# Graph layer on one core: the forward scan's result and a node tile's first residual sum in PSUM in place of SBUF

## What is computed

```
x1  = x + sigmoid(GAT(xn) + bias) + linear_attention(xn) * gate(xn) @ Wproj + bproj
xn2 = layernorm(x1)
out = x1 + xn2 + (FFN(xn2) * score, only for the top half of the nodes by score = xn2 @ wr + br)
```

## Time and profile before

| | |
|---|---|
| time, median of 3 runs | 1304.03 us (1302.03 to 1304.25) |
| the profiled execution, its own time | 1300.92 us |
| its span, first to last instruction | 1299.1 us |
| PE busy | 1033.9 us, 80% |
| DVE busy | 1011.7 us, 78% |
| POOL busy | 834.9 us, 64%, 832 gathers among it |
| ACT busy | 553.2 us, 43% |
| mean granted clock of TensorE | 0.887 of full speed |

### The profile page before, as it was taken

The page is one execution under the profiler, slowest core; times in us unless marked ns, Lnnn a source line. Parts: engine busy times, 40 slices in busy tenths (PEclk is TensorE's granted clock), DMA queues, the critical chain, the costliest instruction groups (busy, mean ns, idle before and its releaser), DMA issues.

```text
span 1299.1 us, 24124 instructions
## 1 busy us (share of the span) xinstructions
PE 1033.9 (80%) x5823; PEld 801.6 (62%) x5823; DVE 1011.7 (78%) x2620; ACT 553.2 (43%) x1169; POOL 834.9 (64%) x876
## 2 busy tenths in 40 slices
PE   4897578675887978779887787889788897788886
PEld 2685456543666756667666665667566675666665
DVE  4783666578778878788888888888788887888788
ACT  1234323133544535454453544535354553535521
POOL 1114666677777777777777777777777777777000
PEclk9898789866979988899888998989888988889789
DMA  9876566666666666656666666666656566666205
GB/s 353 300 153 156 177 186 178 190 161 179 155 161 162 173 164 167 175 157 172 164 166 169 161 172 159 165 160 167 175 154 171 160 168 162 165 163 160 54 1 198
DMA packets 158650, 218.64 MB, mean 168 GB/s; under 512 B 48937, under 2 KB 121437, under 8 KB 158605
## 3 DMA queue, kind: packets, MB, share of 16 engines
q0 software_dynamic: 39984, 110.94, 34.1%
q1 hardware_dynamic: 108976, 96.41, 25.7%
q10 hardware_dynamic: 9645, 10.78, 2.5%
HBM read 174.14 MB, written 43.88 MB: 168 GB/s over the span
## 4 chain that ended last, share of the span: by engine, by line
PE 33%; DVE 15%; issue 13%; POOL 13%; DMA 12%; ACT 2%; SPq 2%; DVEq 1%; POOLq 0%; ACTq 0%
POOL ring L708 13%; PE bank L1900 8%; DMA ring<-feat_d,idx 8%; PE bank L1865 7%; PE bank L1837 7%; DVE ring L1306 4%; PE bank L1816 3%; PE bank L1876 2%; PE bank L1988 2%; DMA parts_d<-wout 2%; PE bank L1825 2%; DVE xnT L1511 1%; PE bank L1699 1%; DMA lists<-dloc_d 1%; DVE lk L1266 1%
## 5 line engine op out<-in xcount | busy, mean ns | idle before, releaser
L708 POOL DMA_INDIRECT ring<-feat_d,idx x832 | 819.0, 984 | 285.5 <-issue 228.3
L1306 DVE TENSOR_TENSOR ring<-ring,bank 128x1024 f32<-128x1024 f32 x208 | 240.0, 1217 | 2.7 <-ACT bank L1579 2.7
L1865 PE MATMUL bank<-ring,hot 128*64 128x265 f32 x1664 | 213.0, 400 | 16.5 <-DVE ring L1306 16.1
L1900 PE MATMUL bank<-late,w_s 128*128 128x256 f32 x768 | 219.1, 443 | 0.4 <-ACT hT L1638 0.4
L1900 PEld LDWEIGHTS bank<-late,w_s 128*128 128x128 f32 x768 | 172.4, 229 | 31.1 <-ACT hT L1638 0.5
L1865 PEld LDWEIGHTS bank<-ring,hot 128*64 128x64 f32 x1664 | 143.7, 140 | 67.5 <-issue 18.2
L1579 ACT ACTIVATE bank<-diff 128x64 f32<-128x64 f32 x52 | 11.8, 228 | 399.3 <-DVE diff L1290 349.4
L1837 PE MATMUL bank<-w_s,hT 128*128 128x256 f32 x720 | 175.9, 400 | 1.2 <-ACT hT L1666 1.2
L1816 PE MATMUL bank<-ident,lk 128*16 128x128 f32 x208 | 43.0, 346 | 154.2 <-DVE lk L1266 154.2
L1837 PEld LDWEIGHTS bank<-w_s,hT 128*128 128x128 f32 x720 | 141.6, 202 | 22.4 <-ACT hT L1666 1.4
L1816 PEld LDWEIGHTS bank<-ident,lk 128*16 128x16 f32 x208 | 17.4, 102 | 170.7 <-DVE lk L1266 131.1
(11 more groups left out here) (268 smaller groups left out, 1620.3 us busy)
## 6 DMA issues: line engine op xcount, KB each, us to landing
parts_d<-zero SPq DMA_DIRECT2D x59, 265.0 KB
parts_d<-wout SPq DMA_DIRECT2D x208, 66.2 KB
lists<-dloc_d SPq DMA_DIRECT2D x104, 128.0 KB
ring<-feat_d,idx POOLq DMA_INDIRECT x832
parts<-parts_d SPq DMA_DIRECT2D x49, 265.0 KB
three<-in_x SPq DMA_DIRECT2D x49, 128.0 KB, 3.1
out<-xnT SPq DMA_DIRECT2D x5, 896.0 KB, 4.2
three<-in_x SPq DMA_DIRECT2D x15, 256.0 KB, 5.5
```

The lines of the kernel that those rows point to most:

```text
L708: pool.indirect_dma_start(out=ring[:, u * TI + q, 0:AW], out_offset=None, in_=feat_d, in_offset=bass.IndirectOffsetOnAxis(ap=idx[:, u, q:q ...
L1306: V.tensor_tensor(feats, feats, ex[:, g * TG:(g + 1) * TG, :].unsqueeze(3) .to_broadcast([P, TG, HEADS, HD]), ALU.mult).then_inc(S("scaled ...
L1865: mm = T.matmul(bank[2 + n][c * WIN:(c + 1) * WIN, 0:SW], hot[:, q, :], ring[:, u * TI + q, 0:SW], start=(j == 0), stop=(j == TG - 1))
L1900: mm = T.matmul(bank[6 + g][:, m % 2 * 2 * P:(m % 2 + 1) * 2 * P], w1_s[:, t, m * P:(m + 1) * P], xn2T[:, t, :], start=(t == 0), stop=(t = ...
```

## The change

The forward scan writes its result back over its input in bank 1, and the backward scan reads it there; the tile `forth` is no longer used in `maxima`. For all node tiles but the last three, x1 is held in `bk_t[:, 256:512]`, the other half of the projection's bank, in place of `sd`: L1385, L1389 and L1393 write it there, and L1389, L1393, L1395, L1348 and L1362 read it there. PE's guards of the bank move accordingly: `turn_scores` and `project` wait for `rest_made` (L1362 of the previous tile) in place of `proj_read`, and for `max_made` in place of `forth_made`. No instruction is added or taken away.

```diff
-                    V.tensor_tensor_scan(forth[:, :], brk[:, 0:GE], bk_t[0:TI, :], LOWEST, ALU.add, ALU.max
+                    V.tensor_tensor_scan(bk_t[0:TI, :], brk[:, 0:GE], bk_t[0:TI, :], LOWEST, ALU.add, ALU.max
                                          ).then_inc(S("forth_made"), 1)
                     dve.wait_ge(S("forth_made"), k + 1)
-                    V.tensor_tensor_scan(srow[:, :][:, ::-1], brk[:, 1:GE + 1][:, ::-1], forth[:, :][:, ::-1],
+                    V.tensor_tensor_scan(srow[:, :][:, ::-1], brk[:, 1:GE + 1][:, ::-1], bk_t[0:TI, :][:, ::-1],
                                          LOWEST, ALU.add, ALU.max).then_inc(S("max_made"), 1)
...
+                def first_sum(i, u):
+
+                    return sd[:, u, :] if isinstance(i, int) and i >= NT - 3 else bk_t[:, C:2 * C]
...
-                    V.tensor_scalar(to, sd[:, u, :], bn[:, u, 6:7], bn[:, u, 9:10], ALU.subtract, ALU.mult
+                    V.tensor_scalar(to, first_sum(i, u), bn[:, u, 6:7], bn[:, u, 9:10], ALU.subtract, ALU.mult
                                     ).then_inc(S("xn2_made"), 1)
...
-                    V.tensor_tensor(tile(xnT, i), sd[:, u, :], to, ALU.add).then_inc(S("rest_made"), 1)
+                    V.tensor_tensor(tile(xnT, i), first_sum(i, u), to, ALU.add).then_inc(S("rest_made"), 1)
...
+                    x1 = first_sum(i, u)
                     dve.wait_ge(S("proj_done"), i + 1)
-                    V.scalar_tensor_tensor(sd[:, u, :], bk_t[:, 0:C], rstd[:, bass.ds(i, 1)], prow[:, :], ALU.mult, ALU.add
+                    V.scalar_tensor_tensor(x1, bk_t[:, 0:C], rstd[:, bass.ds(i, 1)], prow[:, :], ALU.mult, ALU.add
...
-                    V.scalar_tensor_tensor(sd[:, u, :], sa[:, u, :], 0.5, sd[:, u, :], ALU.mult, ALU.add
+                    V.scalar_tensor_tensor(x1, sa[:, u, :], 0.5, x1, ALU.mult, ALU.add
...
-                    V.tensor_tensor(sd[:, u, :], sd[:, u, :], xs[:, u, :], ALU.add).then_inc(S("x1_made"), 1)
+                    V.tensor_tensor(x1, x1, xs[:, u, :], ALU.add).then_inc(S("x1_made"), 1)
                     dve.wait_ge(S("x1_made"), i + 1)
-                    V.bn_stats(bn[:, u, 0:6], sd[:, u, :]).then_inc(S("bn_made"), 1)
+                    V.bn_stats(bn[:, u, 0:6], x1).then_inc(S("bn_made"), 1)
...
                     if isinstance(k, int) and k <= LAG_SUM:
                         if k:
-                            pe.wait_ge(S("forth_made"), k)
+                            pe.wait_ge(S("max_made"), k)
                     else:
-                        pe.wait_ge(S("proj_read"), k - LAG_SUM)
+                        pe.wait_ge(S("rest_made"), k - LAG_SUM)
...
                 def project(i, u):
                     pe.wait_ge(S("prod_made"), i + 1)
-                    if not known_below(i, 1):
+                    if isinstance(i, int) and i > NT - 3:
                         pe.wait_ge(S("proj_read"), i)
+                    elif not known_below(i, 1):
+                        pe.wait_ge(S("rest_made"), i)
                     if not (isinstance(i, int) and i + LAG_SUM >= NI):
-                        pe.wait_ge(S("forth_made"), i + LAG_SUM + 1)
+                        pe.wait_ge(S("max_made"), i + LAG_SUM + 1)
```

## The result

| | before | after |
|---|---|---|
| median (lowest to highest) of 5 runs each | 1304.03 us (1302.03 to 1305.03) | 1288.86 us (1281.69 to 1289.61) |
| ratio after / before, 95% interval | | 0.9872 [0.9844, 0.9899] |
| the profiled execution, its own time | 1300.92 us | 1281.69 us |
| granted clock of that execution | 0.887 | 0.895 |

The change makes the kernel 1.28% faster, 15.2 us between the medians; the interval reaches from 13 to 20 us. The forecast was 1291.5 us, 1285 to 1298, with 91% for faster; it said 12.3 us. The profiled execution of after is the fastest of its five. The other four took 1283.97 to 1289.61 us; the clock was 0.895 in the two shortest and 0.889 or 0.890 in the other three. So its 19.2 us against the profiled execution of before are more than the change brings on average; where the time goes can still be read from it.

The account below looks back on a forecast made before the run. POOL's gathers were taken to pace the 44 steps, stretched by DVE instructions with two SBUF inputs. Removing 17.9 us gross less 5.6 coming back gave 12.3: 1304.0 - 12.3 = 1291.7, stated as 1291.5 us, range 1285 to 1298.

Parts of the forecast that it names:

- What bounds the kernel: In the 44 steps POOL issues gather after gather and hardly waits, so its 20.63 us a step is the loop's period.
- Part 1: Gathers starting under the backward scan L1277 are no longer stretched: 12.1 us in the steps plus 1.0 in the ramp.
- Part 2: Gathers starting under the tile sums L1348, L1393, L1362 and L1389 are no longer stretched: 4.8 us.
- Part 3: Gathers shift under L1332 and L1358 (3.2 us), L1358 starts later (1.2), POOL waits anew (1.2): 5.6 us back, 0 to 10.
- rival 4: Faster: phases of gathers against DVE fall well and only 1 us comes back, about 1287 us; 14%.
- Part 4: DVE durations: PSUM costs scans and sums nothing; L1348 goes from 415 to 480 ns, 3.0 us in all, hidden.
- Part 5: PE's moved guards in turn_scores and project are never the last wait, so they cost nothing.
- Rival 1: Slower: reading and writing one bank takes DVE two turns a column at L1274, L1385, L1389, L1393; about 1328 us; 4%.
- Rival 2: No change: the stretch comes with the scan's time, not its operands; only L1348's 2.1 us go, about 1302 us; 5%.
- Rival 3: Half: gathers slide far more into L1210, L1332 and L1358, 10 us come back, about 1296 us; 17%.

Follow-up runs that it names:

- after_plus: The changed kernel with two more DVE statistics instructions a step, whose output nobody reads; 1297.80 us on chip A, 0.9959 of the kernel before.
- scan_only_2: The kernel before with only the scans changed: forward result kept in PSUM, tile sums still in SBUF; 1293.72 us on chip A, ratio 0.9913.
- guards_only: The kernel before with only PE's waits as the change has them, every tile still in SBUF; 1301.48 us on chip A, ratio 0.9989.
- after_again: The changed kernel as it stands, run again on chip B; 1615.82 us, 1.0205 of the kernel before there.

## Why the prediction was right, point by point

**What bounds the kernel.** Right. POOL's gathers pace the 44 steps: in five of the six traces the window is the gathers' busy time plus 214 to 216 us of fixed gap, and only after_plus, made to run out of DVE's room, departs from it. The share of the span would have pointed at PE.

**Part 1, the scans, 13.1 us gross.** Right: in the 44 steps of scan_only_2 the stretched time is 12.4 us below the kernel before (8.1 below guards_only on the same chip), no gather over 1.21 us was left, and the ratio says 11.3 us, 7 to 15.

**Part 2, the tile sums, 4.8 us gross.** In the stretch of after 45 gathers start under L1352, L1394 and L1398 (none under L1366), and none is stretched, where 49 were in scan_only_2, by 4.2 us. Taken alone its time was not measured on a chip where POOL paces. One reading was wrong: L1348 doesn't have two SBUF tensors like the other three, but one, in a fast form. From PSUM, without that form, it stretches none.

**Part 3, what comes back, 5.6 us.** This is the term that was mis-sized, and why the forecast was 3 us short. By the medians 17.9 - 15.2 = 2.7 us came back, if the gross is taken as counted, and in the profiled execution, the fastest, nothing did. I had the gathers slide under L1332 and L1358 once the long stretches were gone. In scan_only_2 nothing slid. In after L1210, L1332, L1358 (now L1362) and L1328 hold 47 gathers, by 5.4 us, in place of 55 by 9.6: L1362 holds 4 in place of 17, L1332 7 in place of 13, L1210 15 in place of 22, and L1328 21 in place of 3, for 0.05 us each. All that is stretched is 6.0 us, where my terms leave 26.9 - 16.9 + 4.4 = 14.4. POOL's new waits came to less as well: above the fixed gap there are 1.3 us in place of 0.8, so 0.5 us for the 1.2 reckoned, and 1.04 of the 1.3 are one wait before a 15th gather.

Why the dot product came free can be followed in the positions of the gathers, though no run tests it alone. L1352 takes 0.13 us longer than L1348 did, so L1362 starts that much later. In the kernel before, the 17 gathers that L1358 holds start 104 to 155 ns after it, 13 of them at 104 to 111. In after, 7 gathers start 21 to 26 ns ahead of L1362 and 5 start 52 to 91 ns after it, and none of these is held; the 4 that are start 102 to 105 ns after it. So a gather has to start some way into the instruction to be held. At L1332 in after the edge lies between 44 ns (not held) and 45, at L1277 in the kernel before between 8 ns (not held) and 46. I had counted 0.065 us and reckoned that it holds each gather longer. Chance has a part too: in guards_only, with no operand moved, L1358 holds 9 gathers and L1332 9, and the window is 5.1 us shorter than in the kernel before. The 3 us that the forecast missed are no more than such phases do. The effect of a shift has no sign of its own; it depends on whether the next instruction moves over the gather's start or away from it. I had put the better case at 14% as rival 4, 1287, to which 1288.9 lies nearer (1.9 us) than to 1291.5 (2.6). That the time fell so near the forecast is in part luck: the gross was right, what comes back was not.

**Part 4, durations.** L1352 was to take 480 ns and takes 544, 46 x 0.064 = 2.9 us of DVE more than reckoned. Scans and sums were to cost nothing in PSUM and cost next to nothing: L1274 1216 ns for 1207, L1394 and L1398 429 and 432 for 427 and 425. Both were hidden. The wait at L1257 went to 17.7 us where I had said 22, 0.40 a step where I had said 0.5 to 0.6, but not because of them: 22 was 37.3 - 12.3 - 3.0, while the stretch became 18.7 us shorter in this execution, and 37.3 - 18.7 is 18.6. That leaves 0.9 us for the longer instructions. POOL's round shrank more than reckoned; DVE's own, with its waits for PE in it, is 19.8 us in both kernels (20.63 - 0.85 and 20.20 - 0.40).

Of the two pages weighed in the prediction: the 62 cycles that the Trainium skill ("VectorE: DVE Perf Modes", section "The TRN2 errata") adds for a PSUM source don't show in the scans and sums, which lost 9 ns at most. L1352 lost 130, twice that figure, and it is also the one that left a fast form; no run separates the two. The Trainium skill's inference in "SBUF — State Buffer", section "Who interferes with whom", that `tensor_tensor` didn't stall a DMA of GpSimd because descriptor generation needs the write interface, doesn't carry over to these gathers: scan_only_2, where only the scan's operand moved and PE's wait for it with it, has a longest gather of 1.20 us in the 44 steps, guards_only on the same chip one of 1.89.

**Part 5, the waits.** Right, by guards_only.

**The rivals.** Rival 1 (in-place PSUM takes a second turn for each column, 1328) falls by the rows of L1274 and L1398: 9 and 7 ns more where it wanted 527 and 264. Rival 2 (the time of the scan) falls by scan_only_2. Rival 3 (10 us come back) falls by part 3: 2.7 us by the medians.

**The size.** 15.2 us by the medians and 16.7 by the ratio (0.0128 x 1303), against 12.3. The two profiled executions differ by 19.2, of which the clock, 0.895 against 0.887, may hold some; how much wasn't separated.

## What to carry to other kernels

If GpSimd's indirect DMAs pace a loop, lay each gather beside what the vector engine had under way at its start: here an instruction with both inputs in SBUF held it until it ended, and moving one input to PSUM freed it, at 9 ns an instruction, or 130 where the instruction lost a fast form by it. The gross gains counted from the trace held here; what came back through shifted phases was mis-sized, so give that part a range of both signs, and expect it from any edit: 0.84 us of work a step, put into 0.85 us of room, cost 12 us. And read what paces the loop on the chip at hand: on four chips this loop waited for PE, and the gain was gone.

## What was not expected of the hardware

- Chips differ by some 22% for the same kernel: 1303 to 1304 us in the comparison of the prediction and on chip A, 1591 to 1609 on B to E, with a granted clock of 0.82 in place of 0.89 and waits called "remote" of 127 us on POOL alone, on one core that works by itself. Each chip was seen in one session, so it could also be the session. In the timeline of after_again PE's L1821 starts at 1225.38 us with 0.60 us of work, and DVE's L1274, which needs it, only at 1231.01. L1194, ahead of it in DVE's list, ended at 1229.58, and the last 1.43 us are its own wait:

```profile
1225.38 0.60 PE L1821 MATMUL bank<-ident,lk 128*16 128x128 f32 x4 [0.23 <-issue]
1231.01 1.22 DVE L1274 TENSOR_TENSOR_SCAN bank<-brk,bank 16x512 f32<-16x512 f32 x1 [1.43 <-remote]
```

- A second per-partition scalar, with its multiplication, costs L1352 60 ns on 256 columns, in PSUM and in SBUF alike.
- The gathers hold DVE as well. In the kernel before L1257, a copy of 128x16, takes 176 ns in the median and 417 at most, and L1229 175 and 415. The long ones start when a gather has been under way for some 0.52 us or more, and end within 0.01 us of its end; those that start earlier in a gather take 0.16 to 0.20 us.
